# The feed-forward weights' transposes moved behind the next batch's static product

## The chip, the cores and the metric

The kernel runs on one NeuronCore of one Trainium2 chip. The time is the device time of the whole program in microseconds. Before the change three runs took 791.64, 794.45 and 795.36 us, so the median is 794.45 us. The profiled execution took 791.38 us, and its trace spans 789.7 us of that.

## The reference

Two layers stand one behind the other on 16 batches of 512 tokens with 128 channels. Only the first matters here:

```
xn = _layernorm(x)
x = x + _L0_attn_ref(xn, ...) + _L0_ffn_ref(xn, ...)

static_out = x_act @ W.T                      # x_act is xn, W is 128x128
k = _rmsnorm(x_act.reshape(B, L, H, d), k_norm_w)
o_dyn = _gated_delta_rule_scan(q=k, k, v=-static_out, lam, beta)   # 512 steps, 16 heads of 8
h = silu((x @ w1.T) * w1_s) * ((x @ w2.T) * w2_s)                  # 128 -> 512
h = gelu((h @ h1.T) * h1_s);  h = gelu((h @ h2.T) * h2_s)          # 512 -> 512, twice
y = (h @ w3.T) * w3_s                                              # 512 -> 128
```

The second layer is a linear attention with decays and a low-rank correction. The change doesn't touch it.

## The kernel before

The program has two blocks. The first, `prepare`, ends at about 148 us. It goes over the 16 batches and makes for each what the recurrence needs: the normalised input turned round (`xnT`), the keys (`kT`), the static product (`rr`), the couplings between the four tokens of a small block (`coup`), and their solved forms. It also turns the feed-forward weights. The second block runs the recurrence, the feed-forward network and the second layer.

Every engine has its own queue in `prepare`, written out as a loop over turns k. The queues meet only at semaphores. In one turn the engines work on several batches: turn k begins batch k and finishes batch k-3. Per turn, in this order:

- VectorE (DVE): the statistics of batch k (L605, L612), the lower part of weight group k-3 (`lower`, L666), the sums of squares (L628), the first step of the solve of batch k-3 (L265, L269), the factors of the norm of batch k (L617 to L622), the second step, the products of batch k-2 (L649), the third step, the inverse root (L633) and the keys (L638) of batch k-1.
- ScalarE (ACT): the root for batch k (`root`, L477), the copy of the keys (L507), the copy of the turned input (L499), the copy of the static product (L512), the root mean (L494), the factors (L531), the norm (L483), the upper part of weight group k-2 (`upper`, L536), the square (L490), the key squares (L517), and the couplings of batch k-2 (L524).
- TensorE (PE): the static product of batch k-2 (`static`, L773), the couplings' products of batch k-3 (`couplings`, L781), the keys' (L766), the turned input (L758), the factors' product of batch k-3 (`factors`, L791), and the four transposes of weight group k-2 (`weights`, L801).
- GpSimdE (POOL): the scaling and a second solve. SyncE issues the loads and stores.

There are 11 weight groups of four 128x128 squares. Groups 0 to 9 are split in two: `upper` copies the transposes from PSUM to `w_hi` in a rounded format, and `lower` subtracts `w_hi` from the same PSUM tile to get `w_lo`. Group 10 is `w3`, which DVE only scales (`last_weight`, L672).

All this shares one PSUM tile, `ps_f`. The factors' product is written there, then ACT reads it (L531), then the transposes of a weight group are written there, then `upper` and `lower` read them, then the next factors' product comes. So `weights` waits for `fac_ok`, `upper` for `tr_done`, `lower` for `hi_done`, and `factors` for `lo_done`.

The other PSUM tile that matters is `in_ps`. PE writes the couplings' products of a batch there only when DVE has finished all three steps of the solve of the batch before (`r_step`) and the products (`prod_ok`). ACT then copies them to `coup`, behind its key squares.

Of the kernel before, what the change touches and what calls it, by code (L numbers as in the profile page):

```python
# [118 lines left out]
def at(s, stage, *more):  # L119

    if s is not None:
        stage(s, *more)


def prepare(nc, io, scr, c):
# [14 lines left out]
    with ctx:  # L140
# [84 lines left out]
        NG = len(groups)  # L225
# [33 lines left out]
        def earlier(d):  # L259
            return slice(0, (BLK - d) * BSEG)  # L260
# [10 lines left out]
        def arrived(g):  # L271

            if g < 2:
                return mat_in[g], 16
            if g == NG - 1:
                return mat_in[4], 16
            return mat_in[2 + g % 2], 16 * (g // 2)

        def of(n):

            return Sequence(None, n) if 0 <= n < B else None
# [5 lines left out]
        def reuse(eng, done, count):  # L287
            if count > 0:
                eng.wait_ge(done, count)

        with nc.allow_non_contiguous_dma(reason='a few hundred words of scales and per-head factors'), nc.Block() as block:
# [182 lines left out]
            def _(act):  # L474
# [40 lines left out]
                def key_squares(n):  # L515
                    act.wait_ge(kT_ok, n.count(1, 2))
                    act.activation(k2[:, :].rearrange("p (s b i) -> p s i b", i=BLK, b=BSEG),  # L517
                                   kT[n.slot][:, :].rearrange("p (s i b) -> p s i b", i=BLK, b=BSEG), ACT.Square).then_inc(k2_ok, 1)

                def couplings(n):  # L520
                    act.wait_ge(p_step, n.count(SWEEPS, SWEEPS))
                    act.wait_ge(n_mm, n.count(1, 2))
                    for d in range(1, BLK):
                        ins = act.activation(coup[n.slot][:, d - 1, :, earlier(d)], in_ps[:, d - 1, :, earlier(d)], ACT.Copy)  # L524
                    ins.then_inc(coup_ok, 1)
# [8 lines left out]
                def upper(g):  # L534
                    act.wait_ge(tr_done, g + 1)
                    act.activation(c.w_hi[:, NB * g:NB * g + NB, :], ps_f[:, :, :], ACT.Copy).then_inc(hi_done, 1)  # L536

                def exponentials():
                    act.wait_ge(small_in, SMALL)
                    act.activation(work[:, 2:3], par[:, 2:3], ACT.Tanh)  # L540
                    act.activation(work[:, 0:2], par[:, 0:2], ACT.Exp, scale=-1.0).then_inc(exps, 1)

                def static_weights():
                    act.wait_ge(ws_tr, 1)
                    act.activation(c.ws_t[:, :], ps_s[:, 0, :], ACT.Copy).then_inc(ws_ok, 1)
# [28 lines left out]
                act.activation(first_root[:, :], c.eps_ln[:, :], ACT.Sqrt)  # L574
                for k in range(B + 3):
                    at(of(k), root)
                    at(of(k - 2), keys)
                    if k == 1:
                        static_weights()
                    at(of(k - 1), normed)  # L580
                    at(of(k - 2), static)
                    at(of(k - 1), root_mean)
                    at(of(k - 3), factors)
                    if k == B + 1:
                        key_squares(of(B - 1))
                        couplings(of(B - 1))
                    at(of(k), norm)
                    if 0 <= k - 2 < NG - 1:
                        upper(k - 2)
                    at(of(k), square)  # L590
                    if k == 1:
                        exponentials()
                    if k <= B:
                        at(of(k - 2), key_squares)
                        at(of(k - 2), couplings)
# [156 lines left out]
            @block.tensor  # L752
            def _(pe):
                def normed(m):
                    pe.wait_ge(xn_ok, m.count(1, 1))
                    pe.wait_ge(xT_ok, m.count(1, 1))
                    for t in range(NT):
                        ins = nc.tensor.transpose(ps_x[:, t, :], xn[m.slot][:, t, :], c.ident[:, :])  # L758
                    ins.then_inc(x_tr, 1)

                def keys(m):
                    pe.wait_ge(keys_ok, m.count(1, 1))
                    pe.wait_ge(kT_ok, m.count(1, 1))
                    pe.wait_ge(prod_ok, m.count(1, 2))
                    for t in range(NT):
                        ins = nc.tensor.matmul(ps_k[:, t, :], keys_t[:, t, :], c.by_place[:, :], start=True, stop=True)  # L766
                    ins.then_inc(k_tr, 1)

                def static(m):
                    pe.wait_ge(xT_ok, m.count(1, 2))  # L770
                    pe.wait_ge(r_in, m.count(1, 1))
                    pe.wait_ge(ws_ok, 1)
                    nc.tensor.matmul(ps_s[:, :, :].rearrange("p a b -> p (a b)"), c.ws_t[:, :], xnT[m.slot][:, :],  # L773
                                     start=True, stop=True).then_inc(s_mm, 1)

                def couplings(n):
                    pe.wait_ge(prod_ok, n.count(1, 3))
                    pe.wait_ge(coup_ok, n.count(1, 1))
                    pe.wait_ge(r_step, n.count(SWEEPS, 2 * SWEEPS))
                    for d in range(1, BLK):  # L780
                        ins = nc.tensor.matmul(in_ps[:, d - 1, :, earlier(d)], c.head_ones[:, :], prod[:, d - 1, :, earlier(d)],  # L781
                                               start=True, stop=True)
                    ins.then_inc(n_mm, 1)

                def factors(n):
                    pe.wait_ge(k2_ok, n.count(1, 1))
                    pe.wait_ge(lo_done, min(n.off + 1, NG - 1))
                    if n.off >= NG - 1:
                        pe.wait_ge(w3_done, 1)
                    pe.wait_ge(fac_ok, n.count(1, 1))  # L790
                    nc.tensor.matmul(ps_f[:, :, :].rearrange("p a b -> p (a b)"), c.head_ones[:, :], k2[:, :],  # L791
                                     start=True, stop=True).then_inc(f_mm, 1)

                pe.sem_inc(x_tr, 2)
                pe.sem_inc(k_tr, 1)
                pe.sem_inc(n_mm, 1)
                def weights(g):
                    pe.wait_ge(*arrived(g))
                    reuse(pe, fac_ok, g + 1 if g > 0 else 0)
                    for n, square in enumerate(groups[g]):  # L800
                        ins = nc.tensor.transpose(ps_f[:, n, :], square, c.ident[:, :])  # L801
                    ins.then_inc(tr_done, 1)

                pe.wait_ge(const_done, 4)
                pe.wait_ge(ws_in, 16)
                nc.tensor.transpose(ps_s[:, 0, :], nat_ws[:, :], c.ident[:, :]).then_inc(ws_tr, 1)
                for k in range(1, B + 3):
                    at(of(k - 2), static)
                    if k < B + 2:
                        at(of(k - 3), couplings)  # L810
                    at(of(k - 2), keys)
                    at(of(k - 1), normed)
                    at(of(k - 3), factors)
                    if k == B + 1:
                        couplings(of(B - 1))
                    if 0 <= k - 2 < NG:
                        weights(k - 2)
                pe.wait_ge(powers_ok, 1)
                pe.wait_ge(r_in, B + 1)
                for n in range(NT):  # L820
                    ins = nc.tensor.transpose(ps_s[:, n, :], dec_t[:, n * P:(n + 1) * P], c.ident[:, :])
                ins.then_inc(dec_tr, 1)
                for n in range(PEAKS):
                    pe.wait_ge(peak_done, n + 1)
                    ins = nc.tensor.transpose(ps_x[0:1, n, :], peak[:, n:n + 1], c.ident[:, :])
                ins.then_inc(peak_tr, 1)
# [1906 lines left out]
```

## Time and profile before

| | us |
|---|---|
| median of three runs | 794.45 |
| profiled execution | 791.38 |
| span of its trace | 789.7 |
| DVE busy, of the span | 726.9 (92%) |
| PE busy | 701.7 (89%) |
| POOL busy | 642.3 (81%) |
| ACT busy | 599.2 (76%) |
| DVE busy in the first 160 us | 135.95 |
| ACT busy in the first 160 us | 133.52 |
| POOL busy in the first 160 us | 114.91 |
| PE busy in the first 160 us | 102.59 |

The span is one execution on the one core. The first 148 us are `prepare`. There DVE and ACT are both nearly always busy, PE and POOL are not. The granted clock of PE is 1.00 at 2.4 GHz and 0.50 at 1.2 GHz. In the timeline, instructions of one line that follow each other are drawn together (x4), and a bracket at the end of a row is the idle time of that engine before it and what ended it.

### The profile page before, as it was taken

The numbers are of one execution on the slowest core, as the hardware profiler recorded it, in microseconds if no ns is written. First come the engines' busy times: TensorE is split into PE (matmuls) and PEld (weight loads), VectorE is DVE, ScalarE is ACT, GpSimd is POOL, SyncE is SP. The second block draws the span as 40 slices with busy tenths as digits, with TensorE's granted clock in tenths as the row PEclk, the third lists the DMA queues.
The fourth block names the chain that finished last, engine by engine and source line by source line (L and its number), as shares of the span: only waits on it lengthen the run. The fifth ranks groups of instructions, "written<-read, shape, count | busy, mean of one in ns | idle before, by whom it ended". The sixth has DMA issues, their size and how long they took to land.

```text
span 789.7 us, 13063 instructions
## 1 busy us (share of the span) xinstructions
PE 701.7 (89%) x3325; PEld 518.8 (66%) x3325; DVE 726.9 (92%) x2036; ACT 599.2 (76%) x1363; POOL 642.3 (81%) x640
## 2 busy tenths in 40 slices
PE   3767766589999999999999999776799999999998
PEld 2535433368888888888888888652355666666655
DVE  5889898899999999999999999997698888899887
ACT  7989888678888988898988898684676467657631
POOL 3677789697888997979898799657799779889873
PEclk9899999799999999999999999899999999999999
DMA  5688755600520516152161060611523202121001
GB/s 127 201 254 263 235 207 192 182 29 15 125 63 25 122 40 146 40 116 71 40 130 58 23 123 27 169 38 28 181 84 91 67 27 81 54 64 31 1 28 41
DMA packets 139241, 75.75 MB, mean 96 GB/s; under 512 B 74922, under 2 KB 123052, under 8 KB 139180
## 3 DMA queue, kind: packets, MB, share of 16 engines
q1 hardware_dynamic: 138124, 74.58, 33.9%
q10 hardware_dynamic: 1056, 0.52, 0.2%
q8 instruction: 18, 0.29, 0.2%
q14 instruction: 43, 0.35, 0.1%
HBM read 39.86 MB, written 33.55 MB: 93 GB/s over the span
## 4 chain that ended last, share of the span: by engine, by line
DVE 44%; PE 23%; issue 6%; POOL 6%; ACT 1%; DMA 0%; SPq 0%; POOLq 0%; DVEq 0%; ACTq 0%
DVE r_rec L1266 11%; DVE r_gain L1278 9%; DVE r_pg L1252 9%; DVE r_kw L1272 9%; PE f_ps L2422 6%; DVE r_rec L1286 6%; PE f_ps L2423 5%; PE f_ps L2399 3%; POOL l_kv L1665 3%; PE r_rec L2451 1%; PE r_rec L2457 1%; POOL l_wf L1632 1%; PE r_rec L2441 1%; PE f_ps L2430 1%; PE f_ps L2381 1%
## 5 line engine op out<-in xcount | busy, mean ns | idle before, releaser
L1665 POOL TENSOR_TENSOR l_kv<-l_qkv 128x1024 f32<-128x1024 f32 x64 | 124.5, 1948 | 20.8 <-PE f_ps L2423 20.4
L1266 DVE TENSOR_REDUCE r_rec<-r_pg 128x32 f32<-128x288 f32 x256 | 116.0, 453 | 0.6 <-ACT r_pg L1884 0.6
L1278 DVE TENSOR_REDUCE r_gain<-r_kw 128x64 f32<-128x256 f32 x256 | 105.3, 411 | 0.0
L1340 DVE TENSOR_TENSOR l_qs<-f_ps,l_qd 128x1024 f32<-128x1024 f32 x64 | 78.2, 1221 | 25.2 <-PE f_ps L2423 18.5
L2286 PE MATMUL f_ps<-f_hh,w_hi 128*128 128x512 f32 x256 | 101.3, 396 | 0.0
L2286 PE MATMUL f_ps<-f_gh,w_hi 128*128 128x512 f32 x256 | 100.0, 391 | 1.3 <-POOL f_gl L1537 1.2
L1537 POOL TENSOR_TENSOR f_hl<-f_h,f_hh 128x512 fp32r<-128x512 f32 x64 | 80.9, 1302 | 24.5 <-ACT f_hh L1930 24.1
L1545 POOL TENSOR_TENSOR f_g<-f_a,f_b 128x512 f32<-128x512 f32 x64 | 82.6, 1302 | 16.2 <-ACT f_b L1919 16.0
L1537 POOL TENSOR_TENSOR f_gl<-f_g,f_gh 128x512 fp32r<-128x512 f32 x64 | 82.9, 1310 | 0.0
L1347 DVE TENSOR_REDUCE l_o_in<-l_qs 128x128 f32<-128x1024 f32 x64 | 77.2, 1211 | 0.5
L2422 PE MATMUL f_ps<-l_kv,tri 128*128 128x512 f32 x128 | 69.2, 623 | 8.0 <-POOL l_kv L1665 5.2
L2288 PE MATMUL f_ps<-f_hl,w_hi 128*128 128x512 f32 x192 | 75.7, 395 | 0.0
L2288 PE MATMUL f_ps<-f_gl,w_hi 128*128 128x512 f32 x192 | 74.7, 389 | 0.0
L1286 DVE SCALAR_TENSOR_TENSOR r_rec<-r_rec,lam,r_gain 128x64 f32<-128x64 f32 x256 | 73.0, 285 | 0.9 <-ACT r_w L1895 0.9
L2069 ACT ACTIVATE l_qkv<-f_ps 128x384 f32<-128x384 f32 x64 | 31.3, 488 | 53.2 <-PE f_ps L2399 52.9
L2423 PE MATMUL f_ps<-l_kv,tri 128*128 128x512 f32 x128 | 66.4, 601 | 0.0
L1925 ACT ACTIVATE f_gh<-f_g 128x512 fp32r<-128x512 f32 x64 | 40.9, 640 | 29.0 <-POOL f_g L1545 29.0
L2322 PEld LDWEIGHTS f_ps<-w,f_e 128*128 128x128 f32 x512 | 59.6, 192 | 1.2
L2322 PE MATMUL f_ps<-w,f_e 128*128 128x128 f32 x512 | 59.7, 275 | 0.0
L2286 PEld LDWEIGHTS f_ps<-f_gh,w_hi 128*128 128x128 f32 x256 | 48.1, 188 | 12.4 <-POOL f_gl L1537 2.5
L2286 PEld LDWEIGHTS f_ps<-f_hh,w_hi 128*128 128x128 f32 x256 | 49.0, 191 | 10.4
L2399 PE MATMUL f_ps<-l_w_second,l_xnT 128*128 128x384 f32 x128 | 52.3, 490 | 3.4 <-ACT l_qkv L2069 2.1
(227 smaller groups left out, 2099.3 us busy)
## 6 DMA issues: line engine op xcount, KB each, us to landing
scratch_xnT<-p_xnT SPq DMA_DIRECT2D x16, 256.0 KB, 2.3
scratch_K<-p_kout SPq DMA_DIRECT2D x16, 256.0 KB, 2.4
scratch_fac<-p_fac SPq DMA_DIRECT2D x16, 256.0 KB, 2.0
scratch_R<-p_rr SPq DMA_DIRECT2D x16, 256.0 KB, 3.0
scratch_P<-p_pp SPq DMA_DIRECT2D x16, 256.0 KB, 2.3
first_x<-scratch_xnT SPq DMA_DIRECT2D x16, 256.0 KB, 3.6
first_xt<-in_L_attn_x_dram SPq DMA_DIRECT2D x16, 256.0 KB, 2.9
scratch_W<-r_w SPq DMA_DIRECT2D x16, 256.0 KB, 4.1
```

The source lines that it names most:

```text
L1266: dve.tensor_reduce(w_here(g, blk), pg[q][:, at, :, :, :].rearrange("p (v g) i k -> p v g i k", g=G)[:, :, g, :, :], AX.X, ALU.add).then_i ...
L1278: dve.tensor_reduce(of_group(g, gain), of_group(g, kw), AX.X, ALU.add).then_inc(gain_ok, 1)
L1286: dve.scalar_tensor_tensor(out=of_group(g, state[after]), in0=of_group(g, state[q]), scalar=c.lam4[:, :], in1=of_group(g, gain), op0=ALU.m ...
L1340: dve.tensor_tensor(qs[s % 2][:, :].rearrange("p (h v k) -> p h v k", h=H, k=DH), score_banks(s)[:, :, :].rearrange("p a (h v k) -> p (a h ...
L1537: pool.tensor_tensor(lower, full, upper.bitcast(F32), ALU.subtract).then_inc(done, 1)
L1545: pool.tensor_tensor(g_f[:, j, :], a_f[:, j, :], b_f[:, j, :], ALU.mult).then_inc(gate_ok, 1)
L1665: pool.tensor_tensor(dst, k, v, ALU.mult).then_inc(kv_ok, 1)
L2286: nc.tensor.matmul(bank, c.w_hi[:, weights[k], :], upper[k], start=k == 0, stop=False)
L2288: nc.tensor.matmul(bank, c.w_hi[:, weights[k], :], lower[k], start=False, stop=False)
L2322: ins = nc.tensor.matmul(y[:, tokens], e_f[:, k, tokens], c.w3[:, k, :], start=False, stop=t == NT - 1 and k == NB - 1)
L2422: nc.tensor.matmul(to[:, 0, :], c.tri[:, :], kv[s % 2][:, 0, :], start=True, stop=True)
L2423: nc.tensor.matmul(to[:, 1, :], c.tri[:, :], kv[s % 2][:, 1, :], start=True, stop=True).then_inc(tri_mm, 1)
```

## The change

Two stages move, each by a few places in its engine's queue, and with the turn's number adapted. On ACT `upper` goes from behind the norm to behind the root. On PE `weights` goes from the end of a turn, behind the factors' product, to the next turn, behind the static product.

```
                 for k in range(B + 3):
                     at(of(k), root)
+                    if 0 <= k - 3 < NG - 1:
+                        upper(k - 3)
                     at(of(k - 2), keys)
...
                     at(of(k), norm)
-                    if 0 <= k - 2 < NG - 1:
-                        upper(k - 2)
                     at(of(k), square)
...
                 for k in range(1, B + 3):
                     at(of(k - 2), static)
+                    if 0 <= k - 3 < NG:
+                        weights(k - 3)
                     if k < B + 2:
                         at(of(k - 3), couplings)
                     at(of(k - 2), keys)
...
                     at(of(k - 3), factors)
                     if k == B + 1:
                         couplings(of(B - 1))
-                    if 0 <= k - 2 < NG:
-                        weights(k - 2)
```

The queues of DVE, POOL and SyncE stay as they were, instruction for instruction.

On PE, in turns 3 and 4, before: `p_ps_f` is the shared tile, `p_ps_s` the static product, `p_ps_n` the couplings' products.

```order
L791 MATMUL p_ps_f<-p_k,head_ones 128x512 [waits p_fac_ok,p_lo,p_k2_ok]
L801 MATMUL p_ps_f<-ident,p_nat 128x128 [waits p_fac_ok,p_mat_in1]
L801 MATMUL p_ps_f<-ident,p_nat 128x128 x3
L773 MATMUL p_ps_s<-p_xnT,ws_t 128x512 [waits p_ws_ok,p_r_in,p_xT_ok]
L781 MATMUL p_ps_n<-p_prod,head_ones 128x384 [waits p_r_step,p_coup_ok,p_prod_ok]
```

And now, in the same place:

```order
L791 MATMUL p_ps_f<-p_k,head_ones 128x512 [waits p_fac_ok,p_lo,p_k2_ok]
L773 MATMUL p_ps_s<-p_xnT,ws_t 128x512 [waits p_ws_ok,p_r_in,p_xT_ok]
L801 MATMUL p_ps_f<-ident,p_nat 128x128 [waits p_fac_ok,p_mat_in1]
L801 MATMUL p_ps_f<-ident,p_nat 128x128 x3
L781 MATMUL p_ps_n<-p_prod,head_ones 128x384 [waits p_r_step,p_coup_ok,p_prod_ok]
```

The static product has gone ahead of the four transposes. The couplings' products stand behind both, as before.

On ACT, from the norm of one turn to the copy of the keys of the next, before: `w_hi` is the upper part, `p_tr` the transposes' semaphore, `p_stat_ok` that of the statistics.

```order
L483 ACTIVATE p_xn<-p_x,p_nm,p_rstd 128x128 x3
L536 ACTIVATE w_hi<-p_ps_f 128x512 [waits p_tr]
L490 ACTIVATE p_sq<-p_xn 128x512 [waits p_xn_ok,p_ssq_ok]
L517 ACTIVATE p_k<-p_kT 128x8x4x16 [waits p_kT_ok]
L524 ACTIVATE p_coup<-p_ps_n 128x384 [waits p_n_mm,p_p_step]
L524 ACTIVATE p_coup<-p_ps_n 128x8x32
L524 ACTIVATE p_coup<-p_ps_n 128x8x16
L477 ACTIVATE p_std<-p_mv,eps_ln 128x4 [waits p_stat_ok]
L507 ACTIVATE p_kT<-p_ps_k,knw 128x512 [waits p_k_tr,p_p_in,p_small_in,p_kout_ok,p_prod_ok]
```

And now:

```order
L483 ACTIVATE p_xn<-p_x,p_nm,p_rstd 128x128 x3
L490 ACTIVATE p_sq<-p_xn 128x512 [waits p_xn_ok,p_ssq_ok]
L517 ACTIVATE p_k<-p_kT 128x8x4x16 [waits p_kT_ok]
L524 ACTIVATE p_coup<-p_ps_n 128x384 [waits p_n_mm,p_p_step]
L524 ACTIVATE p_coup<-p_ps_n 128x8x32
L524 ACTIVATE p_coup<-p_ps_n 128x8x16
L477 ACTIVATE p_std<-p_mv,eps_ln 128x4 [waits p_stat_ok]
L536 ACTIVATE w_hi<-p_ps_f 128x512 [waits p_tr]
L507 ACTIVATE p_kT<-p_ps_k,knw 128x512 [waits p_k_tr,p_p_in,p_small_in,p_kout_ok,p_prod_ok]
```

The upper part now stands behind the couplings' copy (L524) and the next turn's root, both of which can wait for others.

On DVE nothing moves. These rows stand there before and now, from the statistics of a turn to the first step of its solve (`p_hi` is what `upper` signals):

```order
L612 BN_AGGR p_mv<-p_stats 128x2 [waits p_stat]
L612 BN_AGGR p_mv<-p_stats 128x2 x3
L666 TENSOR_TENSOR w_lo<-p_ps_f,w_hi 128x512 [waits p_hi]
L628 TENSOR_REDUCE p_ssq<-p_sq 128x64 [waits p_rms_ok,p_sq_ok]
L265 TENSOR_TENSOR p_ps_t<-p_ps_n,p_rr 128x384 [waits p_r_step,p_r_in,p_coup_ok]
```

The lower part of a group keeps its place, right behind the statistics on which the root waits.

## Rows read from the trace of the kernel before

**Rows 1.** The page, its first line.

```profile
span 789.7 us, 13063 instructions
```

**Rows 2.** Waits, 0 to 175 us: who waited for whom; us in total, times, longest.

```profile
PE p_ps_f L801 <- ACT p_fac L531: 23.7, 10, 3.6
...
ACT p_coup L524 <- PE p_ps_n L781: 9.4, 7, 1.9
...
DVE p_ps_t L265 <- ACT p_coup L524: 7.1, 5, 2.1
...
ACT p_rr L512 <- DMA scratch_R<-p_rr: 5.0, 7, 1.6
```

**Rows 3.** Timeline of DVE, turns 6 and 7: start, duration, instruction.

```profile
46.07 0.66 DVE L666 TENSOR_TENSOR w_lo<-p_ps_f,w_hi 128x512 fp32r<-128x512 f32 x1
...
47.24 0.56 DVE L265 TENSOR_TENSOR p_ps_t<-p_ps_n,p_rr 128x384 f32<-128x384 f32 x1
...
50.95 0.29 DVE L269 TENSOR_TENSOR p_rr<-p_rr,p_ps_t 128x128 f32<-128x128 f32 x1
...
53.43 0.38 DVE L612 BATCH_NORM_AGGREGATE p_mv<-p_stats 128x2 f32<-128x6 f32 x4
53.73 0.66 DVE L666 TENSOR_TENSOR w_lo<-p_ps_f,w_hi 128x512 fp32r<-128x512 f32 x1
```

**Rows 4.** Timeline of ACT, turns 6 to 8.

```profile
52.83 0.58 ACT L536 ACTIVATE w_hi<-p_ps_f 128x512 fp32r<-128x512 f32 x1
...
56.91 0.31 ACT L477 ACTIVATE p_std<-p_mv,eps_ln 128x4 f32<-128x4 f32 x1
57.10 0.70 ACT L507 ACTIVATE p_kT<-p_ps_k,knw 128x512 f32<-128x512 f32 x1
...
59.19 0.71 ACT L531 ACTIVATE p_fac<-p_ps_f,gate 128x512 f32<-128x512 f32 x1
...
64.25 0.73 ACT L507 ACTIVATE p_kT<-p_ps_k,knw 128x512 f32<-128x512 f32 x1
```

**Rows 5.** Timelines of ACT, PE and DVE: where one engine hands over to another.

```profile
23.14 0.94 ACT L524 ACTIVATE p_coup<-p_ps_n 128x384 f32<-128x384 f32 x3 [1.16 <-PE p_ps_n L781]
...
64.33 1.10 PE L791 MATMUL p_ps_f<-p_k,head_ones 128*128 128x512 f32 x2 [0.16 <-issue]
...
101.94 0.29 DVE L269 TENSOR_TENSOR p_rr<-p_rr,p_ps_t 128x128 f32<-128x128 f32 x1
102.37 1.54 PE L781 MATMUL p_ps_n<-p_prod,head_ones 128*128 128x384 f32 x6 [0.15 <-DVE p_rr L269]
104.00 0.94 ACT L524 ACTIVATE p_coup<-p_ps_n 128x384 f32<-128x384 f32 x3
104.83 0.30 ACT L477 ACTIVATE p_std<-p_mv,eps_ln 128x4 f32<-128x4 f32 x1
```

**Rows 6.** Timeline of PE at the granted clock 0.50.

```profile
20.28 2.77 PE L781 MATMUL p_ps_n<-p_prod,head_ones 128*128 128x384 f32 x6
...
51.54 1.05 PE L801 MATMUL p_ps_f<-ident,p_nath 128*128 128x128 f32 x4 [3.61 <-ACT p_fac L531]
52.38 1.92 PE L773 MATMUL p_ps_s<-p_xnT,ws_t 128*128 128x512 f32 x2
...
110.02 2.90 PE L781 MATMUL p_ps_n<-p_prod,head_ones 128*128 128x384 f32 x6 [1.70 <-DVE p_rr L269]
```

**Rows 7.** Stretches: PE, PEld, DVE, ACT, POOL busy; PE clock; DMA share; GB/s.

```profile
68.00:71.00 3.00, 3.00 (x9) 1.67 (x7) 2.72 (x10) 3.00 (x6) 2.67 (x5) 0.61 0.84 272
...
85.00:88.00 3.00, 2.98 (x8) 1.69 (x9) 2.75 (x12) 3.00 (x7) 0.91 (x2) 0.62 0.98 329
```

**Rows 8.** Timeline of DVE: the solve's first step in turns 3, 12, 13.

```profile
24.11 0.57 DVE L265 TENSOR_TENSOR p_ps_t<-p_ps_n,p_rr 128x384 f32<-128x384 f32 x1 [1.26 <-ACT p_coup L524]
...
98.22 0.56 DVE L265 TENSOR_TENSOR p_ps_t<-p_ps_n,p_rr 128x384 f32<-128x384 f32 x1
...
105.88 0.55 DVE L265 TENSOR_TENSOR p_ps_t<-p_ps_n,p_rr 128x384 f32<-128x384 f32 x1
```

More of the change, by code:

```diff
@@ L576, in _ @@
                     at(of(k), root)
+                    if 0 <= k - 3 < NG - 1:
+                        upper(k - 3)
                     at(of(k - 2), keys)
@@ L587, in _ @@
                     at(of(k), norm)
-                    if 0 <= k - 2 < NG - 1:
-                        upper(k - 2)
                     at(of(k), square)
@@ L808, in _ @@
                     at(of(k - 2), static)
+                    if 0 <= k - 3 < NG:
+                        weights(k - 3)
                     if k < B + 2:
@@ L815, in _ @@
                         couplings(of(B - 1))
-                    if 0 <= k - 2 < NG:
-                        weights(k - 2)
                 pe.wait_ge(powers_ok, 1)
```

## The prediction

> **What bounds the kernel now.** I read the busy shares first, then the list of waits for the preparation, then the timelines of DVE, ACT and PE side by side over two turns. The change touches only the preparation, the first 148 us of a span of 789.7 [rows 1]. What follows starts behind a barrier, so what the preparation loses or gains goes through to the end.
>
> In the list of waits the largest row is the one at which the change aims: PE waits for the factors' copy before the transposes, 23.7 us in ten times [rows 2]. But PE is not what the preparation waits for. DVE is: from the lower part of one turn to that of the next it takes 53.73 - 46.07 = 7.66 us without one idle bracket between [rows 3]. ACT needs 64.25 - 57.10 = 7.15 us for a turn in which it never waits [rows 4]. Only 9.4 us of waiting for the couplings' products reach ACT, and 7.1 us reach DVE [rows 2]. The first steps of the solve in turns 3 and 12 are 98.22 - 24.11 = 74.11 us apart [rows 8]: nine turns of 8.23 us, that is DVE's 7.66 plus about 0.6 of such waits.
>
> **What the change removes and moves.** No instruction is added or taken away, and no DMA is moved: SP's and POOL's queues stay. On PE two instructions of the static product go ahead of the four transposes. On ACT one copy of 0.58 us [rows 4], ten times, goes from behind the norm to behind the next turn's root.
>
> PE first. The static product needs ACT's copy of the turned input and the free `ps_s`, so it can now run about a microsecond before the factors' copy is done. The couplings' products behind it start sooner by what the static product took in that place: 1.92 us at half clock [rows 6], about half of that at full clock. That would shorten ACT's 9.4 us of waiting. It counts only while those products are started by PE's own queue. Below they are started by DVE, so I take nothing for it; nothing and 9.4 us are its ends.
>
> ACT's copy is the part that costs. Before, the upper part of a group was copied at 52.83, done at 53.41, and DVE took the lower part at 53.73 without a wait [rows 3, 4]. Now the copy stands behind the couplings' copy and the root of the next turn. DVE's queue is unchanged, so its lower part must wait for that, and behind the lower part stand the sums, the whole solve, the norm's factors and the products. These in turn release the couplings' products on PE, whose copy on ACT stands ahead of the next root and the next upper part. This is a loop once a turn. Its length from the rows:
>
> - lower part to the end of the last add of the solve: 50.95 + 0.29 - 46.07 = 5.17 [rows 3]
> - to PE's start: 102.37 - 102.23 = 0.14, the six matmuls 1.54, to ACT's start 104.00 - 103.91 = 0.09 [rows 5]
> - couplings' copy to root 104.83 - 104.00 = 0.83 [rows 5]; root to the next instruction 57.10 - 56.91 = 0.19; the upper part 0.58 [rows 4]
> - from the end on one engine to the start on the other, ACT and DVE, 24.11 - 24.08 = 0.03 [rows 5, 8]
>
> The sum is 8.57 us. A second loop goes round by the statistics, on which the root waits: lower part to the end of the aggregates 53.81 - 46.07 = 7.74 [rows 3], then 0.03, 0.19, 0.58 and 0.03 again: 8.57 too. The second doesn't contain PE, so no speed of PE brings a turn below 8.57.
>
> ACT's own turn of 7.15 has then 1.42 us of slack, which covers the longest wait for a store of R, 1.6 us [rows 2], but for 0.2. The factors' product now waits for the lower part: that ends 0.58 + 0.03 + 0.66 = 1.27 us behind the start of the upper part, the product takes 1.10 [rows 5], so it is done at about 2.4, and its copy on ACT is due at 0.58 + (59.19 - 57.10) = 2.67 [rows 4]. At full clock it just fits; at half clock it is about 0.8 us late and takes some of ACT's slack. I take nothing for either; with the slack used up they would cost up to 0.2 and 0.8 us a turn.
>
> **The sum.** Turn 3 is the first with the new order. PE runs there at half clock. The transposes, which lay in idle time before, now come between static and couplings: 52.38 - 51.54 = 0.84 us [rows 6], so the couplings' products start at 21.12 and not at 20.28. From the couplings' copy on ACT to the solve it was 0.94 + 0.03 = 0.97; now it is 0.83 + 0.19 + 0.58 + 0.03, plus 47.24 - 46.07 = 1.17 for lower part and sums [rows 3], together 2.80. So the solve of turn 3 comes 0.84 + 1.83 = 2.67 us later. Nine turns of 8.57 make 77.13 where there were 74.11: 3.02 more. Turn 13 has no upper part and goes at DVE's own pace, 105.88 - 98.22 = 7.66 [rows 8], and the turns behind it have no weights; DVE is the late engine and nothing gives the lag back. That is 5.69 us.
>
> Then the clock. With the granted clock at 0.50 the six couplings' matmuls take 2.90 us and not 1.54 [rows 5, 6], 1.36 more, and in the loop there is nothing to hide them. In turns 4 to 12 of before three such groups fell in a stretch of low clock: the one behind 52.38 [rows 6] and those in the stretches from 68 and from 85 us, where the granted clock was 0.61 and 0.62 [rows 7]. I take three again: 4.08 us. Their ends are none and nine, 0 and 12.2 us. Together 9.8 us: 791.38 + 9.77 = 801.15 for the profiled execution. The median of the runs lies 3.07 us above it, and on that scale the forecast is 804.2 us, 1.2% slower.
>
> One rule speaks for the change. At 51.54 PE runs at half speed after 3.61 us of idleness [rows 6]. The Trainium skill (TensorE: Matmul & The Clock Gate, the section on HAM oscillation) says that idle gaps between groups of matmuls are what makes the clock fall. By it the static product, which now breaks up the long gap, would keep the clock up and the clock's term would be nothing. The trace agrees only in part: at 110.02 PE is at half clock after a gap of 1.70 us [rows 6], and the new loop leaves PE a gap in every turn: the factors' copy is done at 2.67 + 0.71 = 3.4 us [rows 4] and the transposes some 0.6 later, while the couplings' products start at 0.61 + 5.17 + 0.14 = 5.9. That is 1.9 us.
>
> **The rivals.**
> - *The fixed loop alone.* The clock stays up in turns 4 to 12. For it: PE's gaps get shorter than 3.61 us. Against it: the row at 110.02. It gives 794.45 + 5.7 = 800.1. Chance 0.22.
> - *Low clock in most turns.* Six to nine groups at half clock, or the factors' product late too: 5.7 + 7 x 1.36 = 15.2, so 809.7. For it: the gap comes back in each turn. Chance 0.17.
> - *The wait is gone and the turn falls to DVE's own pace.* Place: the couplings' products, started earlier on PE. Price: nine turns of 7.66 are 68.94, 5.2 us under 74.11, so 789.3. It decides as soon as the upper part is copied before DVE has finished the aggregates of its turn. Against it: the root stands ahead of the upper part and waits for just those aggregates. Chance 0.03.
> - *The lag is given back.* DVE comes late to turn 13, but a store or POOL sets the end of the preparation, and less than 4 us arrive. For it: ACT waits 5.0 us for stores of R, some of it in the last turns [rows 2]. Against it: those stores are issued after DVE's solve. It gives 794.45 + 3 = 797.5. Chance 0.08.
> - My forecast, 5.7 plus some two to five groups: chance 0.50, its own range 801 to 807.
>
> **How the numbers follow.** A change of 0.5% is 4 us, about what a measurement of this kernel can tell from none. The forecast, the fixed loop and the low clock are slower by more than that: 0.89, to which the upper end of the case of the lag given back adds 0.02, so 0.91. The rest of that case is within 0.5%: 0.06. Faster is 0.03. The range from 798 to 810 leaves out the faster case, most of the lag given back, and the end of the low clock.
>
> **What would show it.** In the profile after: DVE has an idle bracket before L666, released by ACT's L536, in each of turns 3 to 12, of about 0.9 us at the least; the starts of L666 are 8.57 us apart or, with low clock, near 9.9, and never 7.66. DVE's waits for L524 before L265 are gone. PE's wait for the factors' copy is shorter, with no gain from it. The preparation ends 5.7 us or more later, and the rest of the span is as before. I am wrong if L666 follows L612 without a gap, or if turns are shorter than 8.5 us.

## The result, and the profile after

The changed kernel takes 800.2 us (median of five runs, 799.15 to 801.93) where the kernel before took 793.91 in the same series. The ratio is 1.0092, with a 95% interval from 1.0073 to 1.011: between 5.8 and 8.7 us slower. The forecast was 804.2 us, with 798 to 810 as its range.

The profiled execution has a span of 798.8 us, 9.1 more than before. The recurrence begins, with DVE's first memset (L1289), at 148.43 us before and at 156.82 now. So 8.4 of the 9.1 us are lost in the preparation. The profiled execution of before, 791.38 us, was faster than all five of its timed runs (the lowest is 791.64), so this pair shows a larger distance than the medians do.

The waits of the preparation after, as in [rows 2] (who waited for whom; us in total, times, longest):

```profile
PE p_ps_n L781 <- DVE p_rr L269: 21.4, 15, 3.2
ACT p_coup L524 <- PE p_ps_n L781: 15.9, 14, 3.5
...
DVE w_lo L666 <- ACT w_hi L536: 11.4, 10, 2.9
...
DVE p_ps_t L265 <- ACT p_coup L524: 3.4, 3, 1.3
```

The largest row of before, PE waiting 23.7 us for the factors' copy [rows 2], is gone. A wait that was not there has come: ten times, DVE waits at the lower part for the upper part. PE now waits for DVE, and ACT for PE. DVE's three waits for the couplings' copy that are left come at 128, 135 and 150 us, in turns without weights.

DVE's timeline over one turn, as in [rows 3] (start, duration, instruction, idle before):

```profile
57.96 0.38 DVE L612 BATCH_NORM_AGGREGATE p_mv<-p_stats 128x2 f32<-128x6 f32 x4
59.19 0.69 DVE L666 TENSOR_TENSOR w_lo<-p_ps_f,w_hi 128x512 fp32r<-128x512 f32 x1 [0.85 <-ACT w_hi L536]
...
60.39 0.56 DVE L265 TENSOR_TENSOR p_ps_t<-p_ps_n,p_rr 128x384 f32<-128x384 f32 x1
...
64.10 0.29 DVE L269 TENSOR_TENSOR p_rr<-p_rr,p_ps_t 128x128 f32<-128x128 f32 x1
...
66.58 0.38 DVE L612 BATCH_NORM_AGGREGATE p_mv<-p_stats 128x2 f32<-128x6 f32 x4
67.81 0.69 DVE L666 TENSOR_TENSOR w_lo<-p_ps_f,w_hi 128x512 fp32r<-128x512 f32 x1 [0.85 <-ACT w_hi L536]
```

The two lower parts are 8.62 us apart. Before it was 7.66, with no bracket [rows 3].

PE and ACT in the same turn, as in [rows 4, 5]:

```profile
64.54 1.54 PE L781 MATMUL p_ps_n<-p_prod,head_ones 128*128 128x384 f32 x6 [1.75 <-DVE p_rr L269]
```

```profile
66.17 0.94 ACT L524 ACTIVATE p_coup<-p_ps_n 128x384 f32<-128x384 f32 x3 [0.84 <-PE p_ps_n L781]
67.00 0.30 ACT L477 ACTIVATE p_std<-p_mv,eps_ln 128x4 f32<-128x4 f32 x1
67.20 0.58 ACT L536 ACTIVATE w_hi<-p_ps_f 128x512 fp32r<-128x512 f32 x1
```

Read with DVE's rows this is the loop: the last add ends at 64.39, PE starts at 64.54 and ends at 66.08, ACT copies the couplings from 66.17, the root comes at 67.00, the upper part from 67.20 to 67.78, and DVE's next lower part at 67.81. In each of the first seven turns ACT waits about 0.84 us for PE, PE 1.64 to 1.75 us for DVE, and DVE 0.85 us for ACT. No engine is full, and the turn is longer than the work of any of them.

The second loop of the prediction, the one by the statistics, is just as tight: the aggregates end at 66.96 and the root starts at 67.00. Both loops close at the same root, and no run here separates them.

Over the turns the starts of L666 are 8.62, 8.62, 8.62, 8.62, 8.62, 8.62, 8.63, 8.95 and 9.08 us apart. Before they were 9.00, 7.82, 7.65, 7.66, 9.84, 7.65, 8.30, 7.65 and 9.89.

Two later groups of couplings' products, in turns that have no weights, ran at half clock:

```profile
124.27 2.90 PE L781 MATMUL p_ps_n<-p_prod,head_ones 128*128 128x384 f32 x6 [1.07 <-DVE p_rr L269]
...
145.87 2.90 PE L781 MATMUL p_ps_n<-p_prod,head_ones 128*128 128x384 f32 x6 [3.24 <-DVE p_rr L269]
```

### The profile page after: what moved, and what is told of

It is laid out like the page before. It is cut to its first block, busy times and chain, and to the rows that moved or that the text cites. A ratio compares the mean times of both kernels' runs of the same rounds, so it can differ in the third digit from the quotient of the medians.

```text
span 798.8 us, 13063 instructions
## 1 busy us (share of the span) xinstructions
PE 704.3 (88%) x3325; PEld 517.5 (65%) x3325; DVE 727.8 (91%) x2036; ACT 603.9 (76%) x1363; POOL 642.5 (80%) x640
## 4 chain that ended last, share of the span: by engine, by line
DVE 45%; PE 25%; POOL 4%; issue 4%; ACT 2%; DMA 0%; SPq 0%; POOLq 0%; DVEq 0%; ACTq 0%
DVE r_rec L1266 11%; DVE r_gain L1278 9%; DVE r_pg L1252 9%; DVE r_kw L1272 9%; PE f_ps L2422 7%; PE f_ps L2423 6%; DVE r_rec L1286 6%; PE f_ps L2399 4%; POOL l_kv L1665 2%; PE r_rec L2451 1%; PE r_rec L2457 1%; PE r_rec L2441 1%; PE f_ps L2430 1%; POOL l_wf L1632 1%; DVE l_qs L1340 1%
## 5 line engine op out<-in xcount | busy, mean ns | idle before, releaser
L1266 DVE TENSOR_REDUCE r_rec<-r_pg 128x32 f32<-128x288 f32 x256 | 129.3, 505 | 0.6 <-ACT r_pg L1884 0.6
L1278 DVE TENSOR_REDUCE r_gain<-r_kw 128x64 f32<-128x256 f32 x256 | 118.6, 463 | 0.0
L1286 DVE SCALAR_TENSOR_TENSOR r_rec<-r_rec,lam,r_gain 128x64 f32<-128x64 f32 x256 | 86.5, 338 | 0.1
L1272 DVE TENSOR_TENSOR r_kw<-r_rec,r_kb 128x256 f32<-128x256 f32 x128 | 60.5, 472 | 0.0
L1252 DVE TENSOR_TENSOR r_pg<-r_rec,r_pt 128x256 f32<-128x256 f32 x128 | 60.2, 471 | 0.0
L1272 DVE TENSOR_TENSOR r_kw<-r_rec,first_kb 128x256 f32<-128x256 f32 x128 | 59.7, 467 | 0.0
```

The costliest lines, as they stand in the source:

```text
L1252: dve.tensor_tensor(pg[q][:, at, :, :, 0:DH].rearrange("p (v g) i k -> p v g i k", g=G)[:, :, g, :, :], of_group(g, state[q]).rearrange("p ...
L1266: dve.tensor_reduce(w_here(g, blk), pg[q][:, at, :, :, :].rearrange("p (v g) i k -> p v g i k", g=G)[:, :, g, :, :], AX.X, ALU.add).then_i ...
L1272: dve.tensor_tensor(of_group(g, kw).rearrange("p (v k) i -> p v k i", k=DH), w_here(g, blk).unsqueeze(2).to_broadcast([P, DH, DH, BLK]), b ...
L1278: dve.tensor_reduce(of_group(g, gain), of_group(g, kw), AX.X, ALU.add).then_inc(gain_ok, 1)
L1286: dve.scalar_tensor_tensor(out=of_group(g, state[after]), in0=of_group(g, state[q]), scalar=c.lam4[:, :], in1=of_group(g, gain), op0=ALU.m ...
```

## The experiments

The theory: the loss is a loop of one turn, from DVE's lower part through its solve, PE's couplings' products, ACT's couplings' copy, the root and the upper part back to the lower part. The rivals: PE's new order, the load of ACT, PE's clock. Each run was timed beside runs of the kernel before on its chip, and the ratio is against those.

**Each half of the change alone.** The first keeps only the diff's part on PE, the second only its part on ACT.

> Only the transposes move (PE, behind the next static product); the upper part stays behind the norm on ACT. My theory, that the cost is the loop through ACT's upper part and DVE's lower part: the starts of L666 on DVE go back to 7.66 us apart with no wait for L536, and the time is that of before or up to 3 us less (791 to 795 us), because PE's couplings' products start earlier. Rival, that the transposes in front of the couplings' products delay PE: turns stay near 8.6 us and the time near 800.

> Only ACT's upper part moves (behind the root of the next turn); the transposes stay at the end of PE's turn. My theory: the whole loss is here, L666 starts 8.62 us apart in turns 3 to 12 as in the changed kernel, with a DVE wait of about 0.85 us for L536 in each; 799 to 802 us, perhaps more since the static product again waits behind the transposes. Rival, that PE's order is the cause: within 2 us of the kernel before.

PE's part alone: 792.81 us, ratio 1.0015 (1.000 to 1.003). ACT's part alone: 800.38 us, ratio 1.0107 (1.0088 to 1.0126), as much as the whole change. The lower parts in DVE's timeline, first with PE's part alone:

```profile
31.01 0.66 DVE L666 TENSOR_TENSOR w_lo<-p_ps_f,w_hi 128x512 fp32r<-128x512 f32 x1
38.66 0.66 DVE L666 TENSOR_TENSOR w_lo<-p_ps_f,w_hi 128x512 fp32r<-128x512 f32 x1
```

and with ACT's part alone:

```profile
50.02 0.69 DVE L666 TENSOR_TENSOR w_lo<-p_ps_f,w_hi 128x512 fp32r<-128x512 f32 x1 [0.85 <-ACT w_hi L536]
58.64 0.69 DVE L666 TENSOR_TENSOR w_lo<-p_ps_f,w_hi 128x512 fp32r<-128x512 f32 x1 [0.85 <-ACT w_hi L536]
```

With ACT's part alone eight of the nine turns take 8.61 or 8.62 us. With PE's part alone four take 7.65. Its other five take 8.18 to 9.79 us, as long turns of before did, and their mean over all nine, 8.49 us, is no shorter than the 8.38 of before. Twice ACT waited long for a store of R, 1.23 and 3.12 us, and PE was at half clock behind it. The first time:

```profile
50.93 2.04 PE L773 MATMUL p_ps_s<-p_xnT,ws_t 128*128 128x512 f32 x2 [2.76 <-issue]
...
53.62 2.77 PE L781 MATMUL p_ps_n<-p_prod,head_ones 128*128 128x384 f32 x6
```

So what speaks against PE's order as the cause is the time, and that the bracket before L666 is not there in every turn. That PE's part might give up to 3 us was wrong. In three of the turns the upper part itself waits, since the transposes now stand behind the static product: 1.40 us on ACT in turn 3, and 0.8 us behind each of those two stores.

**The lower part behind the solve's first step**, in the changed kernel:

```diff
                     at(of(k), aggregate)
+                    at(of(k - 1), square_sums)
+                    at(of(k - 3), solve, 0)
                     if 0 <= k - 3 < NG - 1:
                         lower(k - 3)
                     elif k - 3 == NG - 1:
                         last_weight()
-                    at(of(k - 1), square_sums)
-                    at(of(k - 3), solve, 0)
```

> The changed kernel, with DVE's lower part (and the last weight) put behind the sums and the first step of the solve in the same turn. It takes the upper part out of the loop: the solve waits for the couplings' copy alone. My theory: DVE's waits for L536 vanish, turns take 7.7 to 8.0 us, and the time is 790 to 796 us. A small loss may stay, as the factors' product waits for a later lower part and ACT for it. Rival, that the loss is ACT's or PE's order itself and not DVE's wait: 799 to 801 us as the changed kernel.

797.47 us, ratio 1.0069 (1.0047 to 1.0092). The waits for L536 are gone and six of nine turns take 7.75 to 7.93 us. So the loop is open. But the time is 1.5 us above the upper end of what I expected, and its interval overlaps that of the whole change (1.0073 to 1.011). By this run alone, opening the loop is not shown to give much back. Three turns took 8.60, 9.17 and 11.27 us; in the longest ACT waited 2.26 us for a store of R:

```profile
85.31 1.03 ACT L512 ACTIVATE p_rr<-p_ps_s 128x512 f32<-128x512 f32 x1 [2.26 <-DMA scratch_R<-p_rr]
...
91.64 0.94 ACT L524 ACTIVATE p_coup<-p_ps_n 128x384 f32<-128x384 f32 x3 [1.35 <-PE p_ps_n L781]
```

This opened a second question: what lifts the turns above DVE's own pace once the loop is open, the stores or the clock?

**A second copy of the upper part**, in the changed kernel and in the kernel before:

```diff
                     act.wait_ge(tr_done, g + 1)
+                    act.activation(spare[:, :, :], ps_f[:, :, :], ACT.Copy)
                     act.activation(c.w_hi[:, NB * g:NB * g + NB, :], ps_f[:, :, :], ACT.Copy).then_inc(hi_done, 1)
```

> The changed kernel with ACT's copy of each upper part done twice: first into a spare tile, then into w_hi (0.48 us more between starts, ten times). If the copy lies in the loop that sets the turn, L666's starts go from 8.62 to 9.10 us apart, 4.3 us over nine turns and 4.8 with the first: about 805 us. Rival, that ACT's idle time in the turn (0.84 us before the couplings' copy) would take it: turns stay 8.62 us and the time 800 us.

> The kernel before with the same second copy. There the copy stands between the norm and the square, outside of any loop with DVE's lower part, and ACT's turn of 7.15 us grows to 7.63, just under DVE's 7.66. My theory: 0 to 2 us more than before (what little slack ACT had for late stores is gone), against 4.8 us in the changed kernel. Rival, that ACT's load as such sets the turn in both: 4 to 5 us more here too.

In the changed kernel 805.82 us, ratio 1.0166 (1.0143 to 1.0188). In the kernel before 794.64 us, ratio 1.003 (1.0015 to 1.0045). The same ten copies cost 5.9 us in the loop (the ratio 1.0166 less the 1.0092 of the change, of 792 us; the two were measured in different series) and 2.3 us outside it. I had expected 4.8 and at most 2. In the loop the turns went to 9.10 us, as they should, but for two:

```profile
43.49 0.69 DVE L668 TENSOR_TENSOR w_lo<-p_ps_f,w_hi 128x512 fp32r<-128x512 f32 x1 [1.33 <-ACT w_hi L538]
53.95 0.69 DVE L668 TENSOR_TENSOR w_lo<-p_ps_f,w_hi 128x512 fp32r<-128x512 f32 x1 [2.69 <-ACT w_hi L538]
63.05 0.69 DVE L668 TENSOR_TENSOR w_lo<-p_ps_f,w_hi 128x512 fp32r<-128x512 f32 x1 [1.34 <-ACT w_hi L538]
```

The first two are 10.46 us apart. In between PE made the couplings' products at half clock:

```profile
48.84 2.90 PE L783 MATMUL p_ps_n<-p_prod,head_ones 128*128 128x384 f32 x6 [0.90 <-DVE p_rr L270]
```

2.90 against 1.54 is 1.36 us, and 10.46 less 9.10 is 1.36 us. A half-clock group passes whole into such a turn.

**An extra matmul in PE's gap**, first in turns 3 to 16 of the changed kernel, then from turn 4 on:

```diff
                     if 0 <= k - 3 < NG:
                         weights(k - 3)
+                    if 4 <= k < B + 2:
+                        nc.tensor.matmul(ps_x[...], c.ws_t[:, :], xnT[k % 2][:, :], start=True, stop=True)
```

> The changed kernel with one more matmul of 512 columns a turn on PE, ahead of the couplings' products, in the gap where PE waits for DVE; its result is not read. It takes about 0.9 us of the 1.75 us gap. Theory A, that low clock in turns 11 to 17 makes part of the loss: the stretches of low clock vanish and the time is 2 to 3 us less than the changed kernel, 797 to 798 us; turns stay 8.62 us. Theory B, that all the loss is the loop in turns 3 to 12: the time stays at 800 within 1 us.

> As the filler run, but the extra matmul only from turn 4 on, since in turn 3 PE ran at half clock and the filler delayed the loop's start by 2.1 us. Theory A, that low clock behind turn 10 makes 2 us of the loss: 798 us, the start of the recurrence at 154.7 and not at 156.8 us. Theory B, that the clock is no part of it: 800 us.

802.07 us, ratio 1.0125 (1.0104 to 1.0146), and 800.57 us, ratio 1.0098 (1.0074 to 1.0122). Neither is faster than the change. In the first the clock stayed up in turns 4 to 16, but in turn 3 the extra matmul ran at half clock and put the first lower part 2.07 us later. From the first lower part to the recurrence this trace takes 156.77 - 26.78 = 129.99 us and the changed kernel's 156.82 - 24.71 = 132.11. So between these two traces the clock kept up was worth about 2.1 us, and turn 3 took it back. In the second run a turn of 9.54 us shows the same trap:

```profile
55.23 1.06 PE L801 MATMUL p_ps_f<-ident,p_nath 128*128 128x128 f32 x4
56.08 1.56 PE L813 MATMUL p_ps_x<-p_xnT,ws_t 128*128 128x512 f32 x2
57.48 1.46 PE L781 MATMUL p_ps_n<-p_prod,head_ones 128*128 128x384 f32 x6
```

The clock had fallen before the extra matmul, which then stood in front of the couplings' products. By the medians the runs don't settle how much low clock adds to the loss; a filler directly before the work it is to help is the wrong tool for that.

**The same in the kernel before**, in the gap behind the factors' product:

```diff
                     at(of(k - 3), factors)
+                    if 4 <= k <= B:
+                        pe.wait_ge(xT_ok, k + 1)
+                        nc.tensor.matmul(ps_x[...], c.ws_t[:, :], xnT[(k - 1) % 2][:, :], start=True, stop=True)
```

> The kernel before with one extra matmul of 512 columns a turn (turns 4 to 16) on PE, between the factors' product and the transposes, where PE waits 1.8 to 3.7 us for the factors' copy; its result is not read. It tests whether low clock is what lifts the turns of before from DVE's 7.66 to 8.23 us. If so: the half-clock groups of couplings' products in turns 6, 8, 10 and 13 vanish, and the time falls by 2 to 4 us, to 788 to 791. Rival, late stores of R (ACT waits 1.4 and 1.6 us for them in turns 6 and 10) make those turns long: half of it or nothing, 791 to 793 us.

790.86 us, ratio 0.9986 (0.9972 to 1.000): at most 2.2 us, and possibly nothing. Two turns stayed long, 9.39 and 10.14 us; ACT waited 0.93 us for a store of R in the first and 2.64 us in the second. That speaks for the rival, the stores.

**Three tiles for the solved static product**, so that late stores of R hold nobody up:

```diff
-        rr = two("rr", [P, L])
+        rr = [sb(f"rr{u}", [P, L]) for u in range(3)]
...
-                    reuse(act, st_r[m.slot], both(m))
+                    reuse(act, st_r[(m.off + 1) % 2], 32 * ((m.off - 3) // 2 + 1))
```

and `rr[... % 3]` wherever it is read or written. It was run in four forms: in the kernel before, there with the extra matmul, in the changed kernel with the lower part moved, and in the changed kernel.

> The kernel before with three tiles for the static product and its solved form instead of two, so that ACT's copy waits for the store of the batch three back. The 5.0 us that ACT waits for stores of R go. If they are what lifts the turns of before from 7.66 to 8.23 us, the time falls by 2 to 4 us (788 to 790 us). Rival: low clock alone lifts them, and the time stays within 1 us of before.

> The kernel before with both: three tiles, and the extra matmul in PE's gap behind the factors' product (turns 4 to 16). With neither late stores nor low clock all turns 4 to 12 should take DVE's 7.66 us; 4 to 6 us less than before (786 to 788 us). If one of them makes the other harmless, no more than the better of the two alone.

> The changed kernel with the lower part behind the solve's first step, and with three tiles for the static product. The run with the lower part moved alone took 797.5 us with turns of 7.75 to 7.8 us but for three longer ones, in which ACT waited for stores of R or for PE at half clock. If the stores were most of its remaining loss, it comes to 792 to 794 us; if the half clock was, it stays at 796 to 797.

> The changed kernel with three tiles for the static product. In it ACT waits 0.84 us in each turn anyway and a turn is set by the loop of 8.62 us, so my theory says that late stores cost almost nothing: 799 to 800.5 us. A rival, that the stores cost the same everywhere, gives the gain of the kernel before here too, 2 to 4 us.

| kernel | us | ratio (interval) | L666 apart, mean | recurrence begins |
|---|---|---|---|---|
| before, three tiles | 786.63 | 0.9915 (0.9891 to 0.994) | 7.71 | 143.09 |
| the same with the extra matmul | 787.42 | 0.9929 (0.9903 to 0.9954) | 7.80 | 144.03 |
| changed, lower part later, three tiles | 793.18 | 0.9992 (0.9965 to 1.0018) | 7.98 | 147.46 |
| changed, three tiles | 798.22 | 1.0065 (1.0039 to 1.009) | 8.62 | 154.46 |

The first is the fastest of all, 6.4 us under the kernel before it ran beside, more than the 2 to 4 I expected. Eight of its nine turns run at DVE's own pace:

```profile
45.55 0.66 DVE L666 TENSOR_TENSOR w_lo<-p_ps_f,w_hi 128x512 fp32r<-128x512 f32 x1
...
53.20 0.66 DVE L666 TENSOR_TENSOR w_lo<-p_ps_f,w_hi 128x512 fp32r<-128x512 f32 x1
...
60.84 0.66 DVE L666 TENSOR_TENSOR w_lo<-p_ps_f,w_hi 128x512 fp32r<-128x512 f32 x1
```

The clock goes with it. The stretches of the weights' turns (PE, PEld, DVE, ACT and POOL busy, granted clock, DMA share, GB/s), first before:

```profile
22.00:98.00 76.00, 53.71 (x251) 36.24 (x250) 66.39 (x218) 67.12 (x149) 56.84 (x73) 0.92 0.76 242
```

and with three tiles:

```profile
22.00:92.00 70.00, 50.59 (x251) 31.73 (x249) 66.07 (x220) 67.82 (x150) 56.08 (x71) 1.00 0.80 256
```

The granted clock is 1.00 there without any extra matmul, and the extra matmul adds nothing. So in the kernel before the late stores are the first cause of the long turns: ACT waits, PE idles behind it, and in most such turns PE's clock falls too. They are not the only thing that brings the clock down, as the third row shows.

In the changed kernel the three tiles bring about 2 us by the ratios (1.0092 and 1.0065), whose intervals overlap, and its turns stay at 8.62 us: the loop leaves ACT idle long enough to take most of a late store. Against the same kernel without the change, both with three tiles, the change costs 798.22 - 786.63 = 11.6 us. The traces account for it: the first lower part comes 25.25 - 22.05 = 3.20 us later, and nine turns of 8.62 for 7.71 add 8.2; 154.46 - 143.09 is 11.4 us.

The third row says how much of this the opened loop gives back: 798.22 - 793.18 = 5.0 us of the 11.6, and 6.6 us stay. The time is what I expected if the stores were most of the remaining loss of that kernel, but moving the lower part is no clean cure. Six of its turns take 7.76 to 7.92 us and not 7.65. ACT's idle time before the factors' copy, 0.8 us in one turn of the fourth row, is 4.2 us in ten turns here; the factors' product now waits for a later lower part. The other three turns take 8.31 or 8.32 us. In them no store is late, yet PE is at half clock in the static product:

```profile
42.70 1.53 PE L773 MATMUL p_ps_s<-p_xnT,ws_t 128*128 128x512 f32 x2
...
44.88 2.27 PE L781 MATMUL p_ps_n<-p_prod,head_ones 128*128 128x384 f32 x6
```

That answers the second question for the opened loop: both lift its turns, the stores by more (797.47 us without the third tile, 793.18 with it). The traces put the start of its recurrence 4.4 us behind that of the first row; what makes up the rest of the 6.6 us is not shown.

## Why the prediction was right, and where its sizes were off

- *The mechanism, PE not being what the preparation waits for.* Right. The largest wait of the profile went away with no gain, and PE's half of the change moves the time by 0.15%.
- *The loop.* Right: 8.57 us worked out, 8.62 measured in seven turns. It is there with ACT's part alone, its brackets are gone when the lower part comes later, and a second copy lengthens it to 9.10 us. The 0.05 us is the lower part, 0.69 us when it starts from a wait and not 0.66, and rounding. That a faster PE would not shorten it, because of the second loop, no run tests. DVE's bracket was put at about 0.9 us; it is 0.85.
- *The slack of ACT.* Right in the main. Its waits for late stores fell from 5.0 us to 2.0, one of 1.43 us made a turn 0.33 us longer, and the factors' product was in time.
- *The start in turn 3.* Put at 2.67 us, measured 25.91 - 24.11 = 1.80. The 0.84 us for the transposes in front of the couplings' products did not arrive: those products took 1.74 us and not 2.77, since PE's clock rose during them.

```profile
18.54 2.05 PE L773 MATMUL p_ps_s<-p_xnT,ws_t 128*128 128x512 f32 x2 [3.88 <-issue]
20.38 1.06 PE L801 MATMUL p_ps_f<-ident,p_nat 128*128 128x128 f32 x4
21.23 1.74 PE L781 MATMUL p_ps_n<-p_prod,head_ones 128*128 128x384 f32 x6
```

This is in part luck of the one trace. In both traces PE works without a pause from 18.4 or 18.5 us on, and the granted clock rises at about 21.8 us here and at about 24.3 before. In the other runs with this order those products took 2.05 to 2.38 us. With three tiles in both kernels the distance is 26.45 - 23.75 = 2.70 us. What sets the moment of the rise is not shown.

- *The sum over turns 3 to 12.* 5.69 us worked out, 104.29 - 98.22 = 6.07 measured at the solve of turn 12. In it 0.79 us come from two turns of 8.95 and 9.08 us that a late store and half clock made. The sum came so near because the start, 0.87 us too large, and the nine turns, 78.38 us where 77.13 were worked out, nearly cancel.
- *The term for the clock* is the mis-sized one. I took three groups at half clock in turns 4 to 12, 4.08 us; it was a part of one, 2.00 us for 1.54, so 0.46. The three groups of before that I counted were not whole either: by their own rows they took 1.92, 2.77 and 2.56 us for 1.46, 2.87 us in all. The gap of 1.9 us that I worked out was there (1.75), but it did not bring the clock down in turns 4 to 10. By experiment the falls of before hang on late stores, which hold ACT less in the loop; but the clock also fell twice in the loop with the second copy, where ACT waited 0.5 us in all for stores, and three times in the opened loop with three tiles, where it waited for none. Why the clock falls there is open. In the later turns two groups at 2.90 us, where before had one, put most of the lag from 6.07 at turn 14 to 8.4 us at the end of this one trace. Whether that belongs to the change is open; the medians, 6.3 us apart, suggest mostly not, and the last group took 2.90 us with PE's part alone too, but 1.74 in the changed kernel with three tiles.
- *The lag is not given back.* Right: the lag at the solve of turns 12, 13 and 14 is 6.07, 6.06 and 6.07 us.
- *The rival of the fixed loop alone*, 800.1 us, came nearest to the measured 800.2. I gave it 0.22 and should have given it more.
- *The rule on idle gaps.* The reading that went by the Trainium skill (TensorE: Matmul & The Clock Gate, HAM oscillation) gave the better size: the granted clock in the weights' turns is 0.98, before it was 0.92. But the static product in the long gap is not what did it. With PE's part alone it stands there too, and the clock was 0.91; with ACT's part alone it stands behind the gap as before, and the clock was 0.98.

## What to carry to other kernels

Before moving an instruction behind another in its queue, follow what waits for it all the way round: here a copy of 0.58 us was nearly free where it stood (ten more of them cost 2.3 us), and behind the wait for the couplings it closed a loop over three engines that none of their loads shows. The largest wait in a list is not the one that costs: ask which engine never waits, and whether it is ever held up by the one that does. What did lift the turns of the kernel before were late stores on a tile with only two buffers; a third was worth 0.85%.

## What the runs showed of the hardware

- A gap of about 1.75 us on PE in each turn of 8.62 us left the granted clock at 1.00 for seven turns. With half a microsecond more work on ACT in each turn, and the turn at 9.10 us, it fell to 0.50 twice in nine turns.
- PE began to work at 18.4 to 18.5 us after 3.6 to 3.9 us of idleness in two traces. The granted clock was 1.00 again at about 24.3 us in one and 21.8 in the other.
- A half-clock group of the six couplings' matmuls takes 2.90 us for 1.54, and the 1.36 us went whole into the turn where PE lay in the loop.
- The same store of R held ACT for less than 0.65 us in most turns and for up to 3.12 us in others (PE's part alone), at a DMA share of 0.74 to 0.76 over those turns.
